# Attention masks added in 16 small tiles of the array, the experts' low-rank terms as three-part bfloat16 products, and a new order table

## The reference, cut to what matters

```python
x = x + attn_ref(cond_ref(x, cond, ...), ...)      # hyperbolic transformer block, then windowed attention
x = x + ffn_ref(cond2_ref(x, cond, ...), ...)      # modulated linear map, then a mixture of 4 experts
```

```python
mask = (j > i) & (j <= i + W)                      # local window, W = 64, 16 heads
sc = jnp.where(mask, Qb @ Kw / sqrt(16), -inf);  p = softmax(sc)
...
lmask = arange(64)[None, :] <= (arange(Sx) // chunk)[:, None]   # 64 latents, 8 heads, chunk = 4
lsc = jnp.where(lmask, GQ @ GK / sqrt(16), -inf);  lp = softmax(lsc)
```

```python
base = einsum('bsd,fd->bsf', x, Wi)
lora = einsum('bser,efr->bsef', einsum('bsd,erd->bser', x, A), B)
h = relu(base[:, :, None, :] + lora)
out = einsum('bse,bsed->bsd', w, einsum('bsef,df->bsed', h, Wo))
```

## Time and profile before

| | |
|---|---|
| time, median of 3 runs | 1373.74 us (1373.69 to 1374.19) |
| time of the profiled execution | 1374.78 us |
| its span | 1373.0 us |
| PE busy | 1233.8 us, 90% of the span |
| PEld busy | 871.5 us, 63% |
| DVE busy | 903.6 us, 66% |
| ACT busy | 715.6 us, 52% |
| POOL busy | 215.1 us, 16% |

### The profile page before, as it was taken

How to read it: one execution, slowest core, us unless ns; L and a number is a source line. 1 busy time by engine, 2 the same in 40 slices (tenths; PEclk the granted TensorE clock), 3 DMA queues, 4 the chain that set the end, 5 groups by cost and what they waited for, 6 DMA issues and landing times.

```text
span 1373.0 us, 28598 instructions
## 1 busy us (share of the span) xinstructions
PE 1233.8 (90%) x11124; PEld 871.5 (63%) x11124; DVE 903.6 (66%) x3515; ACT 715.6 (52%) x1476; POOL 215.1 (16%) x177
## 2 busy tenths in 40 slices
PE   3867679998999999999999999999999989889786
PEld 1444455665676767767676767676776766667565
DVE  4557778876776959777686949594967754342312
ACT  0256675756656654756475746665575342423221
POOL 1301111012121210212021302121112020101001
PEclk8888899999999999999999999999999999999987
DMA  9310000100000000000000000000000000000000
GB/s 288 91 62 13 24 25 21 32 25 13 13 32 17 29 20 21 28 21 28 13 29 10 24 17 25 17 14 17 14 17 14 16 14 16 2 17 17 2 9 8
DMA packets 27015, 38.29 MB, mean 28 GB/s; under 512 B 3504, under 2 KB 21296, under 8 KB 26880
## 3 DMA queue, kind: packets, MB, share of 16 engines
q1 hardware_dynamic: 25536, 34.90, 7.8%
q10 hardware_dynamic: 1344, 1.57, 0.4%
HBM read 31.77 MB, written 4.29 MB: 26 GB/s over the span
## 4 chain that ended last, share of the span: by engine, by line
PE 59%; DVE 24%; ACT 10%; issue 5%; DMA 1%; POOL 1%; SPq 0%; DVEq 0%; POOLq 0%; ACTq 0%
PE psg L438 35%; PE psq L438 14%; PE pso L438 7%; DVE nm L880 4%; ACT PQ L1324 3%; PE psg L441 3%; DVE TU L877 1%; DVE U L877 1%; DVE JD L893 1%; ACT M L1324 1%; DVE ST L874 1%; DVE sf L874 1%; DVE sf L871 1%; ACT L1324 1%; DMA QK<-in_w_ada 1%
## 5 line engine op out<-in xcount | busy, mean ns | idle before, releaser
L1324 ACT ACTIVATE PQ<-psq 128x1280 f32<-128x1280 f32 (+2 forms) x144 | 215.9, 1499 | 81.8 <-PE psq L438 81.4
L1675 POOL TENSOR_TENSOR R<-R,rhoT 128x512 f32<-128x512 f32 x64 | 82.2, 1285 | 319.3 <-ACT R L1324 319.3
L438 PE MATMUL psg<-zT,WiT 128*128 128x256 f32 x512 | 130.1, 400 | 0.6 <-DVE R L877 0.6
L438 PE MATMUL pso<-PQ,Vg 128*32 128x256 f32 (+2 forms) x2048 | 117.2, 346 | 4.2 <-ACT PQ L1324 4.2
L438 PE MATMUL psq<-QK 32*128 32x128 f32 (+4 forms) x3328 | 120.4, 302 | 0.0
L438 PE MATMUL psg<-WoT,R 128*128 128x256 f32 x512 | 118.2, 383 | 0.0
L438 PEld LDWEIGHTS psq<-QK 32*128 32x128 f32 (+1 forms) x3328 | 91.5, 164 | 37.2 <-issue 37.2
L880 DVE TENSOR_REDUCE nm<-psq 128x16 f32<-128x2048 f32 (+1 forms) x48 | 92.8, 1932 | 32.7 <-PE psq L438 32.5
L438 PEld LDWEIGHTS psg<-zT,WiT 128*128 128x128 f32 x512 | 97.8, 200 | 17.8 <-issue 3.9
L438 PE MATMUL psq<-maskb,identb 128*128 128x320 bf16 (+2 forms) x512 | 98.2, 314 | 10.0 <-DVE nm L880 7.2
L438 PEld LDWEIGHTS psg<-WoT,R 128*128 128x128 f32 x512 | 94.4, 190 | 15.2 <-issue 3.8
(11 more groups left out here) (224 smaller groups left out, 2397.6 us busy)
## 6 DMA issues: line engine op xcount, KB each, us to landing
bcA<-ada_rows SPq DMA_DIRECT2D x16, 384.0 KB, 3.5
bcB<-ada_rows SPq DMA_DIRECT2D x16, 384.0 KB, 3.5
X<-in_x SPq DMA_DIRECT2D x16, 256.0 KB, 4.0
XR<-in_x SPq DMA_DIRECT2D x16, 256.0 KB, 2.7
out<-XR SPq DMA_DIRECT2D x16, 256.0 KB, 2.1
QK<-NMT SPq DMA_DIRECT2D x128, 3.0 KB
WiT<-in_WiT SPq DMA_DIRECT2D x1, 1024.0 KB, 4.9
WoT<-in_WoT SPq DMA_DIRECT2D x1, 1024.0 KB, 7.4
```

The lines of the kernel that those rows point to most:

```text
L438: return e.matmul(o, lhsT, rhs, start=start, stop=stop, skip_group_check=True)
L1324: return e.activation(o, i, func, **kw)
L1675: e.tensor_tensor(R4, R4, rhoT[:, :].unsqueeze(1).broadcast_to([128, 2, 256]), ALU.mult).then_inc(*pool_moe.mark(b, f"r{f}"))
```

## The change

It has four parts.

Masks: each full-array mask matmul becomes four of 32 by 32 (row strip r of identb and of the mask, column strip o of the bank), so a bank's four small matmuls together write its 128 partitions, and the four banks use the four row strips. The 32-row masks are stored once as wide strips, of which each tile takes a shifted window (MQ, MK, ML, MLT in place of MA, MB_, ML, MW, MLT). Groups "a", "b" and lat get 16 small matmuls, "l" and each chunk of loc get two rounds of 16: 208 in a batch in place of 32, and 3328 in all in place of 512.

Low-rank terms: coefficients and B are each split in three bfloat16 parts, and six products of parts are stacked over 96 partitions (LW, LT, Bst in bfloat16). LW takes four DVE steps in place of two and four bfloat16 matmuls in place of two float32r ones; LT is one ACT copy of 96 by 512 in place of two of 64 by 256.

rho: turned in a step of its own ahead of LW's, with a psg bank of its own, by two transposes; ACT copies it in a step of its own.

The order table is new for all five engines. Setup: POOL no longer clears LT, B is loaded 6 times and not 8, and the mask's columns are 1016 and not 960.

```diff
+            def tiles():
+                for i in range(4):
+                    for j in range(4):
+                        yield i, j, slice(32 * i, 32 * i + 32), slice(32 * j, 32 * j + 32)
+            def unit(r):
+                return identb[r, r]
...
                 take(quad, ("a", b), dve_max.at(b, "a"))
                 w.wait_ge(*act_proj.at(b, "gk1"))
-                for i in range(4):
-                    mm(psq[:, i, :].rearrange("p (r n) -> p r n", r=4), identb[:, :],
-                       MA.unsqueeze(1).broadcast_to([128, 4, 128]), True, False)
+                for i, j, r, o in tiles():
+                    mm(psq[o, i, :].rearrange("p (r n) -> p r n", r=4), unit(r),
+                       MQ[r, 96 - 32 * j:224 - 32 * j].unsqueeze(1).broadcast_to([32, 4, 128]), True, False)
...
-                for i in range(4):
-                    mm(psq[:, i, 0:256].rearrange("p (r n) -> p r n", r=2), identb[:, :],
-                       ML.unsqueeze(1).broadcast_to([128, 2, 128]), True, False)
+                for t in range(2):
+                    for i, j, r, o in tiles():
+                        m = 56 - 32 * t - 8 * j
+                        mm(psq[o, i, 0:256].rearrange("p (e t n) -> p e t n", e=2, t=2)[:, :, t, :], unit(r),
+                           ML[r, m:m + 64].unsqueeze(1).broadcast_to([32, 2, 64]), t == 0, False)
...
                     take(quad, ("lc", b, c), act_loc.at(b, f"p{c}"))
-                    for i in range(4):
-                        mm(psq[:, i, 0:320], identb[:, :], MW, True, False)
+                    for q0, n in ((0, 192), (192, 128)):
+                        for i, j, r, o in tiles():
+                            m = 96 - 32 * j
+                            mm(psq[o, i, q0:q0 + n], unit(r), MK[r, m:m + n], q0 == 0, False)
...
-                bank = take(pg, ("lt", b), act_moe.at(b, "rho"))
+                bank = take(pg, ("rho", b), act_moe.at(b, "rho"))
+                w.wait_ge(*dve_moe.at(b, "rh2"))
+                for t in range(2):
+                    last = tr(bank[:, 128 * t:128 * t + 128], rho[:, t:t + 1].broadcast_to([128, 128]))
+                last.then_inc(*pe_moe.mark(b, "rho"))
+                yield
+                bank = take(pg, ("lt", b), act_moe.at(b, "L"))
                 w.wait_ge(*dve_moe.at(b, "lw"))
-                for t in range(2):
-                    mm(bank[:, 128 * t:128 * t + 128], f32r(LW[:, t].rearrange("p s a d -> p (s a d)")), f32r(ident[:, :]),
-                       True, True)
-                    last = mm(bank[:, 256 + 128 * t:384 + 128 * t], rho[:, t:t + 1].broadcast_to([128, 128]), ident[:, :],
-                              True, True)
+                for s in range(2):
+                    for t in range(2):
+                        last = mm(bank[0:96, 256 * s + 128 * t:256 * s + 128 * t + 128],
+                                  LW[:, t, s].rearrange("p a d -> p (a d)"), identb[:, :], True, True)
                 last.then_inc(*pe_moe.mark(b, "lt"))
...
-                        last = mm(ps[:, 256 * j:256 * j + 256], f32r(Bst[:, f0:f0 + 128]), f32r(LT[:, s, :]), False, True)
+                        last = mm(ps[:, 256 * j:256 * j + 256], Bst[:, f0:f0 + 128], LT[:, s, :], False, True)
...
-                yield from chain(s, b, ("hi", "lw"), copy(f32r(hi), lfb), tt(f32r(lo), lfb, hi, ALU.subtract))
+                yield from chain(s, b, ("hi", "r1", "mid", "lw"), copy(part[:, :, 0:3, :], lfb(3)),
+                                 tt(l, l, part[:, :, 0, :], ALU.subtract), copy(part[:, :, 3:5, :], lfb(2)),
+                                 tt(part[:, :, 5, :], l, part[:, :, 3, :], ALU.subtract))
...
+                copy(rhoT[:, :], pg.where["rho", b][:, 0:256]).then_inc(*s.mark(b, "rho"))
                 yield
                 w.wait_ge(*pe_moe.at(b, "lt"))
...
-                for sl in range(2):
-                    r = slice(64 * sl, 64 * sl + 64)
-                    copy(f32r(LT[r, sl, :]), bank[r, 0:256]).then_inc(*s.mark(b, f"L{sl}"))
-                copy(rhoT[:, :], bank[:, 256:512]).then_inc(*s.mark(b, "rho"))
+                copy(LT.rearrange("p s n -> p (s n)"), pg.where["lt", b][0:96, :]).then_inc(*s.mark(b, "L"))
...
-        "kkeekkeekkeeekkekeewwwwwpppwpmwpmepememeeleelkeekkeekkeeekkekeewwwwwpppwmwmeememeeleelkeekkeekkeeekkekeeww",
+        "epmpmeeeeeleeleekeeeeeekkkkkkkwwwwwppwpwmepemepmpmeeeeeleeleekeeeeeekkkkkkkwwwwwppwpwmeememmeeeleeleekee",
```

More of the change, by code:

```diff
@@ L9 @@
 F32 = mybir.dt.float32
-F32R = mybir.dt.float32r
 BF16 = mybir.dt.bfloat16
@@ L40 @@
[L40 to L44, removed]
@@ L234, in program @@
         bg = sb("bg", [128, 4])
-        Bst = sb("Bst", [128, FF])
+        Bst = sb("Bst", [96, FF], BF16)
         X = sb("X", [128, 8, 2, D])
@@ L695, in lat @@
                 w.wait_ge(*rows[b % 2].at(b // 2))
-                for i in range(4):
-                    mm(psq[:, i, 0:256], identb[:, :], MLT, True, False)
+                for i, j, r, o in tiles():
+                    m = 128 - 128 * (j % 2)
+                    mm(psq[o, i, 0:256], unit(r), MLT[r, m:m + 256], True, False)
                 for ee in range(2):
@@ L945, in late @@
                 yield
-                for r in range(8):
+                for r in range(6):
                     w.wait_ge(*loads[f"B{r}"])
                 w.wait_ge(*loads["hsel"])
-                w.wait_ge(*pool_late.at(0, "mask"))
-                yield from chain(s, 0, ("Bh",), copy(f32r(Bh[:, :]), Bf[:, :]))
-                yield
-                yield from chain(s, 0, ("Bl",), tt(Bf[:, :], Bf[:, :], Bh[:, :], ALU.subtract))
-                yield
-                yield from chain(s, 0, ("Bm",), ts(Bf[:, :], Bf[:, :], hsel[:, 1:2], None, ALU.mult))
-                yield
-                yield from chain(s, 0, ("Bst",), stt(f32r(Bst[:, :]), Bh[:, :], hsel[:, 0:1], Bf[:, :], ALU.mult, ALU.add))
+                yield from chain(s, 0, ("Bh", "Bl", "Bm", "Bst"), copy(Bst[:, :], Bf),
+                                 stt(Bf, Bst[:, :], hsel[0:96, 4:5], Bf, ALU.mult, ALU.add), copy(Bst[:, :], Bf),
+                                 stt(Bst[:, :], Bst[:, :], hsel[0:96, 5:6], Bf, ALU.mult, ALU.add))
                 for k in ("b2", "bg", "ltm", "sidx"):
@@ L1804, in allow @@
         return np.where(m, np.float32(0), neg).astype(np.float32)
[L1806 to L1814 removed]
+    p = q[:, None] % 32
+    cols = lambda n, first: np.arange(n)[None] - first
+    m_q = allow((p - cols(224, 96) >= 0) & (p - cols(224, 96) < 64))
+    m_k = allow((cols(288, 96) - p >= 0) & (cols(288, 96) - p < 64))
+    m_l = allow(cols(120, 56) <= p // 4)
+    m_t = allow(p <= cols(384, 128) // 4)
+    hs = np.zeros((128, 6), np.float32)
     hs[:, 0] = (q // 16) % 2 == 0
```

170 lines of the change are left out of this document (83 added, 87 removed).

## The result

The changed kernel takes 1327.3 us (median of 4 runs, 1326.4 to 1329.2) against 1373.7 of the kernel before on the same chip: ratio 0.9665, 95% interval 0.9648 to 0.9681, some 46 us faster. The profiled execution took 1326.44 us with a span of 1324.6. The forecast was 1344 with a range of 1323 to 1367. So the sign and the range held, and 17 us of the gain were not in the sum.

The account below looks back on a forecast made before the run. TensorE's stream was taken to bound the steady part: 39.8 - 9.0 - 2.7 + 4.9 + 4.8 = 37.8 us less stream, less some 1 for LW, gave 30 us of time: 1344 us, range 1323 to 1367.

Parts of the forecast that it names:

- The premise: Steady part, some ten of 16 batches: TensorE's own stream sets the pace, so each microsecond less of it saves one.
- the 13/16 that I took: Stream to time: ten batches give all of a saving and six give half, so 2.3 us a batch x 13.
- the time goes into new waits: Rival, steady part: the new order leaves TensorE waiting half of what it saves, 1359 us; chance 15%.
- 15 x 0.0067: Mask groups "a" and "b": 15 distances between starts of small tiles, 0.0067 us each, within 0.44 us a group.
- the term for weights that stand unhidden: Small-mask groups: the first round's weights, 32 columns, cost TensorE 0.03 us unhidden in each group.
- The way in: Whole-array work ahead of mask groups: the shape change now always comes, 112 x 0.08 = 9.0 us more stream.
- 4.9 + 4.8 = 9.7 us of stream: Low-rank terms: 4.9 us less for unhidden weights in bfloat16, 4.8 us less for LW's matmuls and rho's transposes.
- VectorE's longer LW chain: Routing on VectorE: two more LW steps end it some 0.4 us later; some 1 us was taken off the saving.
- The extra psg bank: rho's extra turn of three banks per batch: covered by other stages' matmuls; uncovered, under 0.6 us a batch.
- 2.7 us against it: New order: 25 more whole-array groups behind a shape change, with float32 weights unhidden, 25 x 0.11 us more.
- the new order gives more: Rival: a batch's whole saving everywhere and a quarter of TensorE's idle time outside the steady part, about 1328 us; 14%.
- The slower rivals: Small tiles: in one row strip they take turns, 1395 us, 5%; or await row neighbours' streams, over 200 us more, 2%.

## Why the prediction was right, and where it was wrong

**The premise was wrong for the order that it was read from, and held for the new one.** It said: "So for some ten of the 16 batches the pace is TensorE's own stream, and a microsecond less of it is a microsecond less of time". That is the step that failed. TensorE was busy 98% of the steady part, and still the chain that ended last went elsewhere for half of the steady time (58 of 72 us in every second batch). The sum would have been too high for that order, as masks and low-rank terms there gave 22 us and not 30, and only 3 of them in six steady batches. What pointed at it was in front of me: 24% VectorE in the earlier trace rows, which the prediction took to agree with its premise. A look at the chain in the steady part by itself would have shown it. The new order puts TensorE on the chain, and there the masks are worth 34.8 us for 42 of stream, a factor of 0.83 for the 13/16 that I took. The rival "the time goes into new waits" is what happened in the old order.

**The masks: mechanism right, size off.** The term "15 x 0.0067" (and "31 x 0.0067") had the distance of float32 pairs for bfloat16 ones. The 16 masks of "a" last 0.43 us in all and their scores start 0.36 after them, where I had said 0.51 and 0.44. Of the 0.08, 0.05 are the distance of starts and 0.03 the term for weights that stand unhidden, which the trace doesn't show: 0.365 - 0.05 - 0.217 leaves 0.10, the remainder alone. With both set right a batch's mask groups take 2.4 us, not 3.11, so the saving is 51 us of stream and not 39.8. With 51 in its place the sum would have been 48 us of stream and 39 of time, 1335; of the 17 us missed this is 9.

**The way in: right.** The last low-rank matmul ahead of a chunk starts 0.12 us after the first of its pair (0.39 less its own 0.27), at 680.35, and the masks at 680.55: the 0.20 that was said. In the same order with whole masks it is 0.11, and behind other whole-array groups 0.31 for 0.22, so the way in costs 0.09 us each time by the start times of both traces.

**Low-rank terms: right in kind.** The prediction had 4.9 + 4.8 = 9.7 us of stream and 8 of time, less 1. Measured are 4.8 us with whole masks and 7.5 with small ones in the new order (both with rho turned by transposes in its own step, so that rho's share of the 4.8 isn't in them), and nothing in the old, where the extra turn of psg took it. Two pairs behind strips take 0.23 us for 0.34 (said: 0.25):

```profile
686.18 0.39 PE L434 MATMUL psg<-LT,Bst 96*128 96x256 bf16 x2
686.41 1.89 PE L434 MATMUL psg<-zT,WiT 128*128 128x256 f32 x8
```

**VectorE's longer LW chain: right to be small.** TensorE's waits for LW fell from 21.4 us to 6.3, with 9.5 for rho beside it, which was turned behind LW before; none of either stands in the six steady batches. No run has VectorE's two steps alone. The rows are of the whole span:

```profile
PE psg L437 <- DVE rho L890: 9.5, 6, 3.1
...
PE psg L434 <- DVE LW L890: 6.3, 4, 1.7
```

**The extra psg bank: right for the new order, priced too low for the old.** The prediction let other stages' work cover it, and put it under 0.6 us a batch without that cover. In the old order, where the cover is gone, the stretch with its waits grew by some 0.9 us a batch, as much as the low-rank form gave. That these waits are the bank's is read from the trace; no run gave rho's turn a bank outside the three.

**The new order: not costed.** The sum had only 2.7 us against it. It is worth 7 us alone, and 24 beside the other parts. The rival "the new order gives more" named about the right time, 1328, and half of the reason: a batch's saving counts nearly in full, but the idle time outside the steady part did not shrink (from the "a" of the twelfth batch to the end TensorE is idle 50 us, for 44). So the sum was short by two things that it didn't hold, shorter groups of tiles (9 us) and what the order gives by itself (7 us). That the wrong premise did no harm was luck: the order happened to mend what it was wrong about, which the prediction nowhere says.

**The slower rivals** fell with the tiles' 3.3 ns. The Trainium skill, "TensorE: Matmul & The Clock Gate", Part 3, gives some 4 ns from start to start of packed tiles, which the bfloat16 tiles bear out (3.3) and the float32 pairs don't (6.7). Its rule in the same part, that weights load beside running matmuls only in other row strips, isn't borne out as it stands: issued four to a row strip or in turn over the strips, the group took the same 0.36 us. (The text of that part also allows a load into a background weight buffer; no run here tells whether that is what the tiles used.)

What stays open: that VectorE's stream holds the old order's stretch at 45.4 us is read from the chain and from the stretch's constant length; no run made VectorE's part shorter by itself. Which of the new table's moves put TensorE back on the chain is open too, since the table was only exchanged as a whole.

## What to carry to other kernels

A busy share of 98% does not say that an engine sets the pace. Read the chain that ended last over the steady part alone: where it leaves the busy engine for tens of microseconds, work taken off that engine there only turns to waiting, until the order is changed so that the chain comes back to it. Cost a new order together with the savings that it exposes, since each alone can look like little (7 us and 21.5 here, and 46 together with the third part). And take a price from rows of the same type: float32 and bfloat16 differed by two in the number that mattered most for the size. Last, a buffer taken from a shared ring is paid by whoever takes the next ones: one more turn of psg ate what the low-rank terms saved, until other work stood between.

## What the runs showed of the hardware

- Matmuls of 32 by 32 tiles start 3.3 ns apart in bfloat16, whether issued along row strips or along column strips, and 6.7 ns apart as float32 pairs; sixteen tiles that each stream 512 columns take 0.36 us to the next group, where four whole-array matmuls of the same columns took 0.96.
- In float32 the second sixteen pairs begin 0.24 us after the first sixteen began: 0.65 us for 32 pairs of 256 columns, against 0.26 for 16 in bfloat16.
- Going over from the whole array to another shape costs about 0.09 us, also into small tiles (0.20 us behind a low-rank group, for 0.11 to masks over the whole array in the same order).
- The granted clock of the steady part is 1.00, the upper level, before and after, with 3328 small matmuls in place of 512 large ones.
